# Identity products in TensorE's prologue, and new lists of steps, in a four-batch RWKV decoder layer

## The chip, the cores and the metric

The kernel runs on one core of one Trainium2 chip. The metric is the device time of one execution in microseconds (us). The kernel before was run three times: 599.24, 600.77 and 601.04 us, median 600.77. One further execution was taken by the profiler. It took 598.28 us, and the span from its first to its last instruction is 596.4 us.

## The reference, cut to what matters

For each of 4 batches of 512 tokens with 512 features, three residual blocks follow each other:

```python
x = x + _L0_attn_ref(_layernorm(x), Wk, Wv, Wr, Wo, tm_k, tm_v, tm_r, time_decay, time_first, ln_g, ln_b)
x = x + _L0_xattn_ref(4, 512, 512, w, u, _layernorm(x), ctx_2048)
x = x + _L0_ffn_ref(_layernorm(x), gate_w, up_w, down_w, gate_s, up_s, down_s)
```

The first block mixes each token with the one before it, projects it with Wk, Wv and Wr, runs the stabilised RWKV recurrence over the tokens (`out = (e1*aa + e2*vt) / (e1*bb + e2)` with running maximum), normalises, gates with the sigmoid of r and projects with Wo. The second runs a like recurrence with the normalised x as key and the context as value. The third is a gated feed-forward layer of 1408 inner features.

## The kernel before

Everything is in one launch, in float32. Each engine has a written list of steps for four stages: `*_FIRST` (the prologue: batch 0, and with a `+` behind the name the first half of batch 1), `*_BODY` (a hardware loop of two rounds), `*_NEXT` and `*_LAST`. In a round the feed-forward part of batch b-1, the second half of batch b's attention work and the first half of batch b+1's run interleaved. An engine runs its list strictly in order. It waits for the others only through semaphores, so a step that is not ready holds up all steps behind it on its engine.

The names that the prediction uses, with their lines:

- PE (TensorE): `turn1` to `turn4` and `return2` and `y` are 16 (for `turn4_0`, `turn4_1`: 8) transposes of 128x128 (L625, L675). `k0` to `k3`, `v0`.., `r0`.. are projections of one block of 128 features over 512 tokens (L636), `wo` is the output projection of all four token blocks (L698). `up0` to `up21` (L722) and `down0` to `down21` (L650) are the feed-forward part. `flag` (L706) is one product whose result chooses the form of the main loop.
- DVE (VectorE): `stat1_k` are the statistics of one half of a batch's x (L980), `stat2_k` those of the recurrence's output (L933), `normN` normalises one block of tokens (L946, L988), `mixk`, `mixv`, `mixr` (L963), `front` (L1014 to L1022), `nv`, `den`, `num`, `part`, `fin` are the recurrence (L1035, L1028, L1041, L1046, L954 and L956), the same with an x in front belong to the second block, `x1_t` and `xf_t` are the residual sums (L1067, L1116), `z4` (L1123) makes the low part of the feed-forward input, `prod` (L1128) and `rest` (L973) belong to the feed-forward part.
- ACT (ScalarE): `share_k` copies and scales a turned block (L778, L810), `rw` scales the normalised output for the gate (L853), `tanh`, `silu`, and `weigh0` to `weigh5`, which sum the low halves of the feed-forward weights.
- SP issues all transfers, on one queue. `words0` to `words2` load gate, up and down from their copies in HBM (L529), each after its copy has landed. `xload0+` and `xload1+` load the two halves of batch 1's x into `mixv` (L494), from which `stat1_0+`, `stat1_1+`, `norm0+`, `norm1+` and `turn1+` start the whole first half of batch 1.

The PSUM banks are four, and are used in turn in the order of PE's list: each use waits until the reader of the use four before it is done. The free accumulators are `gu` (two, for `up`) and `dacc` (two, for `down`).

Of the kernel before, what the change touches and what calls it, by code (L numbers as in the profile page):

```python
# [44 lines left out]
def decoder_layer(nc, x, ctx_t, wk_t, wv_t, wr_t, wo_t, vecs_in, gate_t, up_t, down_t, ffn_scales, down_s, out):  # L45
# [22 lines left out]
    PE_FIRST = """
        turn1 k0 k1 v0 v1 k2 k3 v2 v3 r0 r1 r2 r3 turn2 return2 turn1+ k0+ k1+ v0+ wo v1+ turn3 r0+ r1+
        r2+ r3+ y k2+ k3+ v2+ v3+ turn4_0 flag  # L70
# [33 lines left out]
        norm0 rw2 rw3 norm1 share_k0 share_k1 share_k2 share_k3 share_v0 high2 silu6 silu7 share_v1
        share_v2 share_v3 front0 front1 part0 share_r0 share_r1 sq4 share_r2 share_r3 sq5 high3 norm4
        norm5 part1 silu8 silu9 front2 front3 high4 silu10 silu11 silu12 high5 silu13 part2 part3 silu14
        silu15 high6 xfront0 high7 xfront1 silu16 silu17 xpart0 high8 xpart1 xfront2 xfront3 silu18
        silu19 tanh0 tanh1 tanh2 tanh3 xpart2 high9 xpart3 silu20 silu21 high10 sq6 norm6 z4_0_0 z4_0_1
# [3 lines left out]
        sq7 norm7 silu0 silu1 z4_1_0 z4_1_1 silu2 high0 silu3 high1 norm2 norm3 rw0 rw1 rw2 rw3 silu4  # L112
        sq4 silu5 norm4 high2 sq5 silu6 silu7 norm5 xfront0 xfront1 silu8 silu9 xpart0 high3 silu10
        high4 silu11 xpart1 high5 silu12 silu13 xfront2 xfront3 silu14 high6 silu15 high7 silu16 silu17
        silu18 silu19 xpart2 xpart3 high8 silu20 silu21 high9 sq6 high10 norm6 z4_0_0 z4_0_1
# [11 lines left out]
        nv3 part2 den3 num3 part3 fin2 fin3 stat2_0 stat2_1 norm2 norm3 stat1_0+ stat1_1+ norm0+ rw0 rw1
        rw2 norm1+ mixk0+ mixk1+ mixk2+ mixk3+ mixv0+ mixv1+ mixv2+ mixv3+ front0+ rw3 front1+ den0+
        mixr0+ mixr1+ mixr2+ mixr3+ nv0+ num0+ part0+ den1+ x1_0 x1_1 x1_2 x1_3 fin0+ norm4 nv1+ norm5
        num1+ xfront0 part1+ xin0 xden0 fin1+ xnum0 xfront1 xpart0 xin1 xden1 xfin0 xnum1 xfront2 xpart1  # L130
        xden2 xin2 xfin1 xnum2 xfront3 xpart2 xin3 xden3 xnum3 xpart3 xfin2 xfin3 xf_0 xf_1 xf_2 xf_3
# [16 lines left out]
        norm7 prod0 z4_1_0 z4_1_1 prod1 prod2 stat2_0 stat2_1 prod3 rest0 norm2 norm3 rw0 rw1 rw2 rw3
        prod4 x1_0 x1_1 prod5 norm4 x1_2 rest1 rest2 x1_3 norm5 prod6 prod7 xfront0 xfront1 xin0 xden0
        xnum0 xin1 prod8 prod9 xpart0 xden1 xnum1 rest3 xpart1 prod10 prod11 xfin0 rest4 xfront2 rest5  # L150
        xfin1 prod12 prod13 xfront3 out0 out1 xin2 prod14 prod15 xden2 rest6 xnum2 prod16 rest7 prod17
        xpart2 xden3 prod18 xin3 xnum3 prod19 xpart3 xfin2 xfin3 rest8 xf_0 xf_1 rest9 prod20 prod21
# [1040 lines left out]
```

## Time and profile before

| | us |
|---|---|
| median of three runs | 600.77 |
| the profiled execution | 598.28 |
| its span | 596.4 |
| prologue, to the first `up` | 165.3 |
| first and second round of the loop | 136.7 each |
| `*_NEXT`, to the first `up` of `*_LAST` | 87.5 |
| `*_LAST` with the end | 70.2 |

The boundaries of the stages are the starts of `up0` on PE. "Busy" is the time in which an engine works, and the PEclk column of the windows is the granted TensorE clock as a share of 2.4 GHz: 0.50 is 1.2 GHz.

### The profile page before, as it was taken

What the parts mean: (1) busy time and instruction counts of PE and PEld (TensorE: products, weight loads), DVE (VectorE), ACT (ScalarE), POOL (GpSimd) and SP (SyncE); (2) the same over time, 40 slices, a digit from 0 to 9 for tenths busy, and PEclk for the clock granted to TensorE, in tenths of its full rate; (3) what the DMA queues carried; (4) which work ended last, traced back from release to release, by engine and by line L of the source; (5) the groups of instructions that cost most, each with busy time, mean ns of one, the idle gap of its engine ahead of it and who ended that gap; (6) DMA issues with size and microseconds to landing.
All of it is one profiled execution on the core that took longest, in us unless ns stands there. A gap on an engine that the chain in (4) does not pass through costs nothing.

```text
span 596.4 us, 8018 instructions
## 1 busy us (share of the span) xinstructions
PE 536.3 (90%) x2658; PEld 381.6 (64%) x2658; DVE 457.1 (77%) x742; ACT 345.4 (58%) x546; POOL 53.4 (9%) x155
## 2 busy tenths in 40 slices
PE   2998589677799999999889999999969999999995
PEld 2443444323398446885689446786768699989994
DVE  5999778996977489999857589999856499852433
ACT  4737783467868257676557447766644486634221
POOL 2000300101022003000103003000011100000000
PEclk9999699988989999999979999999979999999998
DMA  8999700012100000001060000001040010010001
GB/s 304 414 315 385 291 0 2 18 35 87 48 26 2 1 1 0 1 19 53 1 213 0 0 0 1 0 18 53 0 142 0 1 38 36 0 36 1 2 36 38
DMA packets 14261, 39.02 MB, mean 65 GB/s; under 512 B 1232, under 2 KB 1232, under 8 KB 14032
## 3 DMA queue, kind: packets, MB, share of 16 engines
q1 hardware_dynamic: 14224, 38.57, 18.0%
q8 instruction: 18, 0.29, 0.2%
q14 instruction: 19, 0.16, 0.1%
HBM read 34.37 MB, written 12.85 MB: 79 GB/s over the span
## 4 chain that ended last, share of the span: by engine, by line
issue 38%; PE 34%; DVE 15%; POOL 6%; ACT 5%; DMA 1%; DVEq 0%; POOLq 0%; SPq 0%; ACTq 0%
PE gu L722 13%; PE dacc L650 7%; PE bank L636 6%; PE bank L698 5%; PE bank L625 3%; POOL t_rstd L598 2%; DVE t_slot L954 2%; DVE t_st L1091 1%; ACT L745 1%; DVE t_slot L1099 1%; DVE t_otile L1149 1%; DVE t_slot L1046 1%; POOL t_veps L596 1%; ACT t_z L799 1%; DVE t_xf L1116 1%
## 5 line engine op out<-in xcount | busy, mean ns | idle before, releaser
L722 PE MATMUL gu<-t_z4h,t_gate 128*128 128x256 f32 x352 | 94.1, 299 | 7.9 <-DVE t_z4l L1123 7.5
L722 PE MATMUL gu<-t_z4l,t_gate 128*128 128x256 f32 x352 | 89.3, 286 | 0.0
L722 PE MATMUL gu<-t_z4l,t_up 128*128 128x256 f32 x352 | 89.3, 286 | 0.0
L722 PE MATMUL gu<-t_z4h,t_up 128*128 128x256 f32 x352 | 89.2, 285 | 0.0
L879 ACT ACTIVATE t_h<-gu,t_fsc 128x256 f32<-128x256 f32 x88 | 40.4, 472 | 67.3 <-PE gu L722 65.8
L722 PEld LDWEIGHTS gu<-t_z4h,t_gate 128*128 128x128 f32 x352 | 68.4, 194 | 12.7 <-issue 10.4
L650 PE MATMUL dacc<-t_down,t_hh 128*128 128x512 f32 x176 | 72.5, 412 | 1.8 <-DVE t_hl L973 1.8
L722 PEld LDWEIGHTS gu<-t_z4l,t_gate 128*128 128x128 f32 x352 | 68.3, 194 | 2.4 <-issue 1.7
L650 PE MATMUL dacc<-t_down,t_hl 128*128 128x512 f32 x176 | 69.0, 392 | 0.0
L1128 DVE SCALAR_TENSOR_TENSOR t_h<-gu,t_fsc,t_h 128x256 f32<-128x256 f32 x88 | 40.6, 476 | 36.0 <-ACT t_h L879 35.9
L722 PEld LDWEIGHTS gu<-t_z4h,t_up 128*128 128x128 f32 x352 | 68.1, 193 | 0.0
L722 PEld LDWEIGHTS gu<-t_z4l,t_up 128*128 128x128 f32 x352 | 68.0, 193 | 0.0
L636 PE MATMUL bank<-t_mixk,t_wk 128*128 128x512 f32 x128 | 58.6, 607 | 3.6 <-DVE t_mixk L963 3.3
L745 ACT ACT_TABLE_LOAD x45 | 57.7, 1283 | 1.5 <-PEq L1187 0.7
L636 PE MATMUL bank<-t_mixv,t_wv 128*128 128x512 f32 x128 | 56.7, 592 | 0.0
L698 PE MATMUL bank<-t_wo,t_tanh_r 128*128 128x512 f32 x128 | 55.6, 592 | 0.0
L636 PEld LDWEIGHTS bank<-t_mixk,t_wk 128*128 128x128 f32 x128 | 24.0, 193 | 35.8 <-issue 28.8
L636 PEld LDWEIGHTS bank<-t_mixv,t_wv 128*128 128x128 f32 x128 | 24.3, 190 | 29.0 <-issue 28.7
L698 PEld LDWEIGHTS bank<-t_wo,t_tanh_r 128*128 128x128 f32 x128 | 24.1, 190 | 29.4 <-issue 28.2
L954 DVE TENSOR_TENSOR t_slot<-t_slot 128x1024 f32<-128x1024 f32 x32 | 38.9, 1216 | 2.5 <-ACT t_slot L866 1.4
L650 PEld LDWEIGHTS dacc<-t_down,t_hh 128*128 128x128 f32 x176 | 33.1, 188 | 11.0 <-issue 5.5
L761 ACT ACTIVATE t_hh<-t_h 128x512 fp32r<-128x512 f32 x44 | 27.5, 625 | 20.0 <-PE dacc L650 10.1
(129 smaller groups left out, 930.5 us busy)
## 6 DMA issues: line engine op xcount, KB each, us to landing
t_mixv<-in_x SPq DMA_DIRECT2D x8, 512.0 KB, 6.0
t_xres<-in_x SPq DMA_DIRECT2D x8, 512.0 KB, 5.5
t_ctxt<-in_ctx_t SPq DMA_DIRECT2D x16, 256.0 KB, 2.8
out<-t_otile SPq DMA_DIRECT2D x16, 256.0 KB, 2.2
gate_words<-in_gate_t SPq DMA_DIRECT2D x1, 2816.0 KB, 17.1
up_words<-in_up_t SPq DMA_DIRECT2D x1, 2816.0 KB, 24.3
t_gate<-gate_words SPq DMA_DIRECT2D x1, 2816.0 KB, 15.5
down_words<-in_down_t SPq DMA_DIRECT2D x1, 2816.0 KB, 23.1
```

Of the source, the lines that this page charges most:

```text
L596: pool.tensor_tensor(veps[:, half(k)], var[:, half(k)], small[:, EPSILON, half(k)], ALU.add).then_inc(veps_done, 1)
L598: pool.tensor_tensor(rstd[:, half(k)], veps[:, half(k)], small[:, MINUS_HALF, half(k)], ALU.pow).then_inc(rstd_done, 1)
L625: done = pe.transpose(bank_of(b, s, m)[:, k * P:(k + 1) * P], src[:, k, m * P:(m + 1) * P], ident[:, :])
L636: last = pe.matmul(bank_of(b, s, c)[:, :], w[:, k, c * P:(c + 1) * P], src[:, k, :], start=(k == 0), stop=(k == C - 1))
L650: last = pe.matmul(dacc[j][:, :], as_read(part[:, u % 4, j * P:(j + 1) * P], exact), as_read(down[:, i, :], exact), start=(i == 0 and part ...
L698: done = pe.matmul(bank_of(b, s, m)[:, :], tanh_r[:, k, m * P:(m + 1) * P], wo[:, k, :], start=(k == 0), stop=(k == C - 1))
L722: last = pe.matmul(gu[u % 2][:, side, :], as_read(w[:, k, i * P:(i + 1) * P], exact), as_read(part[:, k, hf * HALF:(hf + 1) * HALF], exact ...
L745: act.preload_act_table_set(name)
L761: act.activation(pair(hh, p), pair(h, p), ACT.Copy).then_inc(hh_done, 1)
L879: act.activation(h[:, u % 4, :], gu[u % 2][:, 0, :], ACT.Silu, scale=fsc[:, 0, u % NI:u % NI + 1]).then_inc(silu_done, 1)
L954: dve.tensor_tensor(slot[:, c % 2, 2:4, :], both, slot[:, c % 2, 0:1, :].to_broadcast([P, 2, T]), ALU.mult).then_inc(square, 1)
L1128: dve.scalar_tensor_tensor(out=h[:, u % 4, :], in0=gu[u % 2][:, 1, :], scalar=fsc[:, 1, u % NI:u % NI + 1], in1=h[:, u % 4, :], op0=ALU.mu ...
```

## The change

PE's prologue list gets 27 steps `warm0` to `warm26`. Each is five products of the identity with itself, 128x128 in float32, into the accumulator `gu[1]`, which nothing reads there; they wait for nothing beside the identity. All lists of PE, ACT and DVE are laid out anew, in all stages; POOL's `*_NEXT` changes by one swap; on SP `words2` now stands ahead of `xload0+` and `xload1+`, and in the loop the loads of x stand first. DVE's `rw` steps get one more wait, for the `tanh` of the same block. No arithmetic that reaches the output is added or removed.

```diff
     PE_FIRST = """
-        turn1 k0 k1 v0 v1 k2 k3 v2 v3 r0 r1 r2 r3 turn2 return2 turn1+ k0+ k1+ v0+ wo v1+ turn3 r0+ r1+
-        r2+ r3+ y k2+ k3+ v2+ v3+ turn4_0 flag
+        warm0 warm1 turn1 warm2 k0 k1 v0 v1 v2 k2 k3 v3 r0 r1 r2 r3 warm3 turn2 warm4 warm5 warm6 warm7
...
     SP_FIRST = """
-        words1 xload0+ xload1+ words2 ctx2 ctx3
+        words1 words2 xload0+ xload1+ ctx2 ctx3
...
     SP_BODY = """
-        ctx0 ctx1 rload0 rload1 xload0 xload1 ctx2 ctx3 out0 out1 out2 out3
+        xload0 xload1 ctx0 ctx1 rload0 rload1 ctx2 ctx3 out0 out1 out2 out3
...
+                elif kind(s) == "warm":
+
+                    for _ in range(5):
+                        pe.matmul(gu[1][:, 0, 0:P], ident[:, :], ident[:, :], start=True, stop=True)
...
                     need(dve, lnt_done, b, c + 1)
+                    need(dve, tanh_done, b, c + 1)
```

SP's queue in the prologue, after the copies of gate and up have been issued. In brackets stand the semaphores that a transfer waits for; before:

```order
L529 DMA t_gate<-gate_words 128x4x1408 [waits gate_raw]
L525 DMA down_words<-in_down_t 64x11264
L529 DMA t_up<-up_words 128x4x1408 [waits up_raw]
L494 DMA t_mixv<-in_x 128x2x512 [waits newv_done] x2
L529 DMA t_down<-down_words 128x11x512 [waits down_raw]
```

and now:

```order
L532 DMA t_gate<-gate_words 128x4x1408 [waits gate_raw]
L528 DMA down_words<-in_down_t 64x11264
L532 DMA t_up<-up_words 128x4x1408 [waits up_raw]
L532 DMA t_down<-down_words 128x11x512 [waits down_raw]
L497 DMA t_mixv<-in_x 128x2x512 [waits newv_done] x2
```

The two halves of batch 1's x now stand behind the load of down, and behind its wait for the copy of down.

PE from `turn2` of batch 0 to the end of the prologue; the products with `t_ident` alone are the new steps, `t_zt` is the recurrence's output, `t_wo`, `t_wk`, `t_wv`, `t_wr` are the weights. Before:

```order
L625 MATMUL bank<-t_ident,t_zt 128x128 x16
L625 MATMUL bank<-t_ident,t_z 128x128 x16
L625 MATMUL bank<-t_ident,t_mixv 128x128 x16
L636 MATMUL bank<-t_mixk,t_wk 128x512 x8
L636 MATMUL bank<-t_mixv,t_wv 128x512 x4
L698 MATMUL bank<-t_wo,t_tanh_r 128x512 x16
L636 MATMUL bank<-t_mixv,t_wv 128x512 x4
L625 MATMUL bank<-t_ident,t_z 128x128 x16
L636 MATMUL bank<-t_xf,t_wr 128x512 x16
L625 MATMUL bank<-t_ident,t_z 128x128 x16
L636 MATMUL bank<-t_mixk,t_wk 128x512 x8
L636 MATMUL bank<-t_mixv,t_wv 128x512 x8
```

and now, from `return2` on:

```order
L628 MATMUL bank<-t_ident,t_z 128x128 x16
L710 MATMUL gu<-t_ident 128x128 x5
L628 MATMUL bank<-t_ident,t_mixv 128x128 x16
L701 MATMUL bank<-t_wo,t_tanh_r 128x512 x16
L639 MATMUL bank<-t_mixk,t_wk 128x512 x8
L639 MATMUL bank<-t_mixv,t_wv 128x512 x8
L710 MATMUL gu<-t_ident 128x128 x15
L628 MATMUL bank<-t_ident,t_z 128x128 x16
L710 MATMUL gu<-t_ident 128x128 x35
L639 MATMUL bank<-t_xf,t_wr 128x512 x16
L639 MATMUL bank<-t_mixk,t_wk 128x512 x8
L639 MATMUL bank<-t_mixv,t_wv 128x512 x8
```

`wo` moved ahead of `k0+`, and `k2+` to `v3+` moved ahead of `y`, which (with 16 transposes of `t_z`) now follows them, then 25 identity products, `flag`, `turn4_0` and the last 10.

DVE at the second half of `stat2` of batch 0 (`t_stats<-bank`), with batch 1's x in `t_mixv`. Before:

```order
L933 BN_STATS t_stats<-bank 128x6 x2
L938 MEMSET t_scrap 128x1
L940 BN_AGGR t_mv<-t_stats 128x2 x2
L946 TENSOR_SCALAR t_z<-bank,t_rstd,t_nmr 128x512 x2
L980 BN_STATS t_stats<-t_mixv 128x6 x2
```

and now:

```order
L940 BN_STATS t_stats<-bank 128x6 x2
L945 MEMSET t_scrap 128x1
L947 BN_AGGR t_mv<-t_stats 128x2 x2
L987 BN_STATS t_stats<-t_mixv 128x6 x2
L989 MEMSET t_scrap 128x1
L991 BN_AGGR t_mv<-t_stats 128x2 x2
L953 TENSOR_SCALAR t_z<-bank,t_rstd,t_nmr 128x512 x2
```

The statistics of batch 1's first half (`stat1_0+`) now stand ahead of `norm2` and `norm3` of batch 0.

## Rows read from the trace of the kernel before

**Rows 1.** Windows: the stages; busy us (instructions) of each engine, clock, DMA share, GB/s

```profile
60.00:79.00 19.00, 11.00 (x45) 8.89 (x46) 12.03 (x30) 13.15 (x17) 4.92 (x16) 0.64 0.59 221
79.00:107.30 28.30, 28.30 (x66) 12.06 (x67) 24.40 (x38) 18.47 (x33) 2.70 (x7) 1.00 0.00 1
107.30:165.10 57.80, 39.49 (x106) 17.84 (x104) 51.62 (x70) 37.98 (x51) 2.86 (x10) 0.89 0.16 54
165.30:302.00 136.70, 130.68 (x664) 94.22 (x664) 115.81 (x185) 86.70 (x137) 15.08 (x36) 0.97 0.04 13
302.00:438.70 136.70, 130.75 (x665) 94.31 (x665) 112.44 (x181) 83.70 (x135) 14.57 (x36) 0.97 0.09 31
438.70:526.20 87.50, 86.80 (x552) 74.11 (x553) 61.20 (x106) 51.84 (x85) 8.26 (x26) 0.98 0.09 31
```

**Rows 2.** DMA issues: size, median us from issue to landing

```profile
t_up<-up_words SPq DMA_DIRECT2D x1, 2816.0 KB, 22.9
t_down<-down_words SPq DMA_DIRECT2D x1, 2816.0 KB, 17.2
```

**Rows 3.** Timeline of SP's queue: start us, duration of the issue

```profile
38.79 0.38 SPq L529 DMA_DIRECT2D t_up<-up_words  x1
51.86 0.89 SPq L494 DMA_DIRECT2D t_mixv<-in_x  x2
54.53 0.37 SPq L529 DMA_DIRECT2D t_down<-down_words  x1
```

**Rows 4.** The tile `mixv`, 45 to 80 us: landing of batch 1's two halves

```profile
DMA to landing us min/median/max: 11.2/11.7/12.1
```

**Rows 5.** Timeline of DVE around `norm3` and `stat1_0+`, and one scan

```profile
67.11 0.81 DVE L946 TENSOR_SCALAR t_z<-bank,t_rstd,t_nmr 128x512 f32<-128x512 f32 x1 [0.66 <-POOL t_nmr L601]
67.83 1.27 DVE L980 BATCH_NORM_STATS2 t_stats<-t_mixv 128x6 f32<-128x512 f32 x2
69.31 1.25 DVE L980 BATCH_NORM_STATS2 t_stats<-t_mixv 128x6 f32<-128x512 f32 x2
98.61 1.23 DVE L1028 TENSOR_TENSOR_SCAN t_st<-t_fade,t_slot 128x512 f32<-128x512 f32 x1
```

**Rows 6.** Timeline of PE: `return2`, `wo`, `v1+`, `r1+`

```profile
67.97 3.25 PE L625 MATMUL bank<-t_ident,t_z 128*128 128x128 f32 x14 [0.96 <-DVE t_z L946]
89.94 13.90 PE L698 MATMUL bank<-t_wo,t_tanh_r 128*128 128x512 f32 x32
103.67 3.60 PE L636 MATMUL bank<-t_mixv,t_wv 128*128 128x512 f32 x8
117.82 5.40 PE L636 MATMUL bank<-t_xf,t_wr 128*128 128x512 f32 x8 [2.86 <-DVE t_slot L1073]
```

**Rows 7.** Timeline of ACT: `rw0` to `rw3` of batch 0, `share_k0+`

```profile
71.64 2.77 ACT L853 ACTIVATE t_z<-bank,t_half_b,t_half_g 128x512 f32<-128x512 f32 x4
76.89 0.69 ACT L778 ACTIVATE t_mixk<-bank,t_vecs 128x512 f32<-128x512 f32 x1 [1.78 <-PE bank L625]
```

**Rows 8.** Waits of DVE, 107.3 to 165.1 us: us in total, times, longest

```profile
DVE t_slot L1014 <- PE bank L636: 2.9, 1, 2.9
DVE t_slot L954 <- ACT t_slot L866: 1.4, 1, 1.4
```

**Rows 9.** Page, groups: the first part of a `fin`

```profile
L954 DVE TENSOR_TENSOR t_slot<-t_slot 128x1024 f32<-128x1024 f32 x32 | 38.9, 1216 | 2.5 <-ACT t_slot L866 1.4
```

**Rows 10.** Timeline of DVE at the end of the prologue: the flag, `norm7`

```profile
163.77 0.14 DVE L1142 TENSOR_SCALAR t_general<-gu 1x1 int32<-1x1 f32 x1
170.02 0.55 DVE L946 TENSOR_SCALAR t_z<-t_xf,t_rstd,t_nmr 128x512 f32<-128x512 f32 x1 [1.20 <-POOL t_nmr L601]
```

**Rows 11.** Windows: the first 3.9 us of the first round

```profile
165.30:169.20 3.90, 3.89 (x18) 3.90 (x19) 3.45 (x4) 3.87 (x6) 0.94 (x2) 0.50 0.02 6
```

**Rows 12.** Timeline of PE: transposes of `y` in the first round; `up0` of the loop

```profile
289.37 1.47 PE L625 MATMUL bank<-t_ident,t_z 128*128 128x128 f32 x12
165.31 0.55 PE L722 MATMUL gu<-t_z4h,t_gate 128*128 128x256 f32 x1 [2.43 <-DVE t_z4l L1123]
```

More of the change, by code:

```diff
@@ L68, in decoder_layer @@
     PE_FIRST = """
-        turn1 k0 k1 v0 v1 k2 k3 v2 v3 r0 r1 r2 r3 turn2 return2 turn1+ k0+ k1+ v0+ wo v1+ turn3 r0+ r1+
-        r2+ r3+ y k2+ k3+ v2+ v3+ turn4_0 flag
+        warm0 warm1 turn1 warm2 k0 k1 v0 v1 v2 k2 k3 v3 r0 r1 r2 r3 warm3 turn2 warm4 warm5 warm6 warm7
+        warm8 return2 warm9 turn1+ wo k0+ k1+ v0+ v1+ warm10 warm11 warm12 turn3 warm13 warm14 warm15
+        warm16 warm17 warm18 warm19 r0+ r1+ r2+ r3+ k2+ k3+ v2+ v3+ y warm20 warm21 warm22 warm23 warm24
+        flag turn4_0 warm25 warm26
         """.split()
     PE_BODY = """
-        up0 up1 turn4_1 up2 turn2 up3 up4 up5 return2 down0 up6 down1 turn1 up7 wo k0 k1 v0 k2 k3 down2
-        v1 down3 down4 up8 up9 down5 v2 v3 up10 up11 down6 down7 up12 up13 down8 down9 down10 turn3 up14
-        up15 down11 r0 up16 up17 up18 down12 down13 r1 up19 r2 r3 down14 down15 up20 down16 up21 down17
+        up0 up1 turn4_1 up2 turn2 up3 up4 down0 return2 up5 down1 down2 turn1 up6 up7 k0 k1 v0 v1 k2 k3
+        down3 wo v2 v3 up8 r0 r1 r2 down4 turn3 down5 up9 up10 up11 down6 down7 up12 up13 r3 down8 down9
+        down10 up14 up15 up16 down11 down12 down13 up17 up18 up19 up20 down14 down15 down16 up21 down17
         y down18 down19 down20 down21 turn4_0
@@ L104, in decoder_layer @@
[L104 to L108, printed above, removed]
+        sq7 silu0 norm7 silu1 z4_1_0 z4_1_1 silu2 silu3 high0 norm2 norm3 silu4 high1 rw0 rw1 rw2 rw3
@@ L109, in decoder_layer @@
         """.split()
     ACT_NEXT = """
[L112 to L115, printed above, removed]
+        sq7 norm7 silu0 silu1 z4_1_0 z4_1_1 high0 silu2 silu3 high1 norm2 norm3 silu4 silu5 rw0 rw1 rw2
@@ L127, in decoder_layer @@
[L127 to L131, printed above, removed]
@@ L132, in decoder_layer @@
-        front2+ norm6 front3+ den2+ nv2+ num2+ part2+ nv3+ den3+ num3+ weigh part3+ flag z4_0_0 z4_0_1
-        fin2+ fin3+
+        stat1_0 stat1_1 norm0 norm1 mixk0 mixk1 mixk2 mixk3 mixv0 mixv1 mixv2 mixv3 front0 front1 nv0
+        den0 num0 nv1 part0 mixr0 den1 fin0 num1 front2 mixr1 part1 nv2 mixr2 mixr3 fin1 front3 den2
+        num2 nv3 part2 den3 num3 part3 fin2 fin3 stat2_0 stat2_1 stat1_0+ norm2 norm3 stat1_1+ norm0+
+        norm1+ rw0 rw1 rw2 rw3 mixk0+ mixk1+ mixk2+ mixk3+ mixv0+ x1_0 x1_1 mixv1+ mixv2+ mixv3+ mixr0+
@@ L134, in decoder_layer @@
+        mixr1+ mixr2+ mixr3+ x1_2 x1_3 norm4 front0+ norm5 front1+ den0+ nv0+ num0+ part0+ nv1+ den1+
+        num1+ part1+ fin0+ xfront0 fin1+ xin0 xfront1 xden0 xnum0 xin1 xpart0 xden1 xnum1 xpart1 xfin0
+        xfront2 xfin1 xin2 xfront3 xden2 xnum2 xpart2 xin3 weigh xden3 xnum3 xpart3 xfin2 xfin3 front2+
+        front3+ den2+ nv2+ nv3+ num2+ xf_0 xf_1 part2+ xf_2 den3+ num3+ norm6 xf_3 part3+ flag z4_0_0
+        z4_0_1 fin2+ fin3+
         """.split()
     DVE_BODY = """
-        norm7 prod0 z4_1_0 z4_1_1 prod1 prod2 rest0 stat2_0 stat2_1 prod3 norm2 norm3 stat1_0 prod4
@@ L143, in decoder_layer @@
-        xfront2 xfin1 xfront3 rest7 rest8 xin2 xden2 xnum2 prod18 xpart2 xin3 xden3 xnum3 prod19 xpart3
-        rest9 xfin2 xfin3 prod20 prod21 xf_0 xf_1 rest10 out2 norm6 xf_2 out3 z4_0_0 xf_3 z4_0_1
+        norm7 prod0 prod1 z4_1_0 z4_1_1 prod2 stat2_0 stat2_1 prod3 rest0 norm2 norm3 stat1_0 stat1_1
+        rest1 norm0 norm1 prod4 prod5 mixk0 mixk1 mixk2 mixk3 rw0 mixv0 mixv1 rw1 front0 mixv2 mixv3
+        front1 den0 nv0 num0 part0 rw2 rw3 den1 nv1 num1 part1 mixr0 mixr1 fin0 front2 fin1 front3 x1_0
@@ L145, in decoder_layer @@
         """.split()
     DVE_NEXT = """
[L148 to L152, printed above, removed]
+        norm7 prod0 z4_1_0 z4_1_1 prod1 prod2 stat2_0 stat2_1 prod3 rest0 norm2 norm3 rest1 rw0 rw1 rw2
```

68 lines of the change are left out of this document (39 added, 29 removed).

## The prediction

> **What bounds the kernel now.** I read the windows by stage first [rows 1]. In the two rounds of the loop PE is busy for 130.7 of 136.7 us, in the next stage for 86.8 of 87.5 us: there PE is the bound, and a new order can only win back 6.0 us a round. The prologue is another matter. From 79.0 to 107.3 us PE never rests, from 107.3 to 165.1 us DVE is busy for 51.6 of 57.8 us and PE for 39.5, and from 60 to 79 us no engine is above 13.2 of 19 us, with the clock at 0.64: a chain that goes back and forth between DVE, POOL, ACT and PE. Its waits name what the change aims at: after 107.3 us DVE waits 2.9 us once for a projection (L1014 [rows 8]), since `y` stands ahead of `k2+`, and 1.4 us for ACT.
>
> **What the clock costs now.** PE's 14 transposes of `return2` take 3.25 us, 0.23 each [rows 6]; 12 in the loop take 1.47 us, 0.12 each [rows 12]. The first window of the loop is at 0.50, 1.2 GHz, after 2.4 us of rest [rows 11, 12]. At full clock it would save half of 3.9 us, 1.9 us. After a rest of 2.86 us, 8 passes of `r1+` take 5.40 us, against 3.60 [rows 6].
>
> **The price of the 27 groups.** No row shows an identity product. A float32 product goes through PE in two passes (the 16 products of `wo` are 32 rows); 8 passes of 512 columns start within 103.67 - 89.94 = 13.73 us / 32 each, 0.43 us, so 128 columns cost 0.107 us, and a transpose of that width 0.12. A group of ten passes is 1.1 us at full and 2.2 us at half clock: I take 1.1. All 27 are 30 us of PE, hidden where PE waits anyway; each is followed below.
>
> **The sum, step by step.** Times are of the profiled execution (598.28 us, span 596.4), which is 2.5 us under the median of the runs.
>
> 1. *Batch 1's x comes later.* Before, up landed at 38.79 + 22.9 = 61.7 us, the halves of x at 51.86 + 11.2 = 63.1 and about 52.3 + 12.1 = 64.4, down at 54.53 + 17.2 = 71.7 us [rows 2 to 4]. So the one queue delivers in the order of issue, and down took 7.3 us of it. `words2` can't be issued before 54.53, as it waits for its copy. With x behind it, down lands at 61.7 + 7.3 = 69.0 and x at 70.4 and 71.7 us.
>
> 2. *DVE waits there, with batch 0 behind it.* `turn2` ends near 61 to 63 us, and two `stat2` steps of 1.5 us are done by 66 even at half clock, so all that the new order and `warm3` gain before it is lost in this wait. `stat1_0+` starts at 70.4, takes 69.31 - 67.83 = 1.5 us, then `norm2` and `norm3` follow: 71.9 and 72.6, done at 73.4 us. Before, `norm3` was done at 67.9 [rows 5]. That is 5.5 us late. `warm4` to `warm8` (5.5 us) lie in the hole and cost nothing; after them PE rests for some 6 us, so `return2` is at half clock again.
>
> 3. *To `share_k0+`.* `return2` 3.3 us, four `rw` on ACT 2.7 us [rows 6, 7]: 79.5 us; `warm9` lies beside the `rw` steps. Then come the last nine or ten transposes of `turn1+`: 1.1 us at full clock, 2.3 at half. 80.6 to 81.8; in the middle 81.2, against 76.89 before [rows 7]: 4.3 us late, so 1.2 have come back.
>
> 4. *`wo` first.* `wo` needs the turned blocks 0 and 1, 2.3 us on, then 15 products of 0.86 us, then four projections of 3.43 us: `v1+` ends 28.9 us after `share_k0+`, at 110.1 us; before, at 103.67 + 3.43 = 107.1. DVE stands idle for the `wo` result and for `k0+` meanwhile, which before it did not need to.
>
> 5. *From `nv1+` to the feed-forward input.* Before, this part had 51.6 us of DVE work in 57.8 [rows 1]. Now `den1+` (1.2) and `fin0+` (1.2 + 0.7) are still to come [rows 5, 9] and `norm5` (0.5) is done: 54.2 us. The waits of 2.9 and 1.4 us go, since `k2+` to `v3+` now come ahead of `y`. PE has room: `turn3` ends near 115, `warm13` to `warm19` (7.7 us) near 122.5, and the last `r+` waits for DVE near 134 in any case; four projections behind it end near 152, when DVE needs `v3+` near 153. With 0.5 us of small gaps the low part is ready at 110.1 + 54.2 + 0.5 = 164.8 us; before 165.1. The 5.5 us of loss and the reordering's gain cancel.
>
> 6. *Into the loop.* `turn4_0` is followed by `warm25` and `warm26`, 2.2 us, which end with the low part. But the read of the flag's result stands behind them in PE's queue, and from that result (163.77 + 0.14 [rows 10]) to `up0` (165.31 [rows 12]) took 1.4 us. So `up0` starts near 166.1, 0.8 us late, at full clock. It then saves 1.9 us, of which most is lost again at `turn4_1`, behind `up1`: it needs `norm7`, done at 170.6 us [rows 10], whose own chain from `xf_3` is about as late as before. Net -0.2 us (-1 to +1).
>
> 7. *Loop, next, last.* The work is the same, PE's rest is 6.0 us a round, nearly all at the end of it, in the chain from `y` over `xf_1` and `norm6` to `up0`; that chain keeps its steps. Walking the new lists, `down0` and `return2` come close behind their inputs (I count 1 us of new waits a round) and the 0.7 us around `y` and the last `down` steps go. I take +0.2 a round (-1.5 to +1.5), -0.1 for the rest. The wait added to `rw` is always met: ACT did `tanh` long before.
>
> Sum: -0.2 + 0.4 - 0.1 = +0.1 us: 598.4 us for a profiled execution, 600.9 as a median. This kernel's runs differ by 0.3%, 1.8 us, so that is the bound of "same". The likeliest case's own range is 599.0 to 602.6.
>
> **Rivals.**
>
> *A. x is not held up* (0.10). If the two transfers share the engines in another manner, or down is copied earlier, the 5.5 us of step 2 go, and with them the half clock of `return2` (14 x 0.11 = 1.6 us) and the wait of up to 1.2 us in step 3: about 8.3 us faster, 592.5. For it speaks only that nothing else in the new order is placed as if x were late; against it all four landings [rows 2 to 4]. The Trainium skill ("DMA: Bandwidth & Descriptors", Queues, rings and completion order) says that transfers of one issuing engine need not complete in the order of issue. No landing of this trace shows that.
>
> *B. The new order gains in the loop* (0.23). The 6.0 us of rest a round shrink by 1.5, the clock in step 6 gives its whole 1.9: -3.0 - 1.7 = -4.7, 596.0; half of that is enough for "faster". For it: DVE is at 115.8 and 112.4 of 136.7 us, so its order has room [rows 1].
>
> *C. Groups at half clock in the way* (0.25, the other side). Ahead of `y` PE waits for `nv2+` and `nv3+` with no group to bridge it, about 2.5 us, as long as the rest that brought 1.2 GHz before `r1+` [rows 6]. Then `y` takes 1.5 us more, and `warm20` to `warm24`, begun late and up to 2.2 us each until the clock is back, end 2 us after `norm6` is ready; `turn4_0` stands behind them. With step 3 at its upper end (+0.6) and 1 us of small waits: +3.6, 604.5. It decides from +1.8 us, when the groups end 1.2 us too late.
> The Trainium skill ("TensorE: Matmul & The Clock Gate", Part 4, PE-mode transpose) says that transposes do not count as busy for the clock. The trace leans to it: clock 0.64 over 60 to 79 us with PE busy 11.0 of 19 us, mostly on transposes [rows 1]. Here that rule would put step 3 at 81.8 and the total at 601.5.
>
> *D. As summed* (0.42).
>
> **Chances.** Faster by over 0.3%: A, B and little else, 0.33. Same 0.42. Slower: C, 0.25. The range of 8 in 10 leaves out A's end and C's upper tail: 595.0 to 604.5.
>
> **What the changed profile would show.** SP's queue: x issued near 55, landing near 70 and 72. DVE: `stat1_0+` waits some 6 us for the transfer of x, `norm3` near 72.6; if it starts near 64, step 1 is wrong and A holds. ACT: `share_k0+` near 81. PE: `v1+` ends near 110, no wait of DVE for `k2+`, groups of 1.1 us, `up0` near 166 with PEclk 1.00 in the first 4 us. The rounds: 136 to 138 us. If `turn4_0` starts right behind the last group of `warm24`, more than 1 us after `norm6`, C holds.

## The result, and the profile after

| | before | after |
|---|---|---|
| median of 20 runs each, us | 599.83 | 602.11 |
| lowest to highest | 597.96 to 601.82 | 600.55 to 606.52 |
| ratio, 95% interval | | 1.0047 [1.0032, 1.0062] |
| the profiled execution, its span | 598.28, 596.4 | 602.58, 600.7 |

The kernel after is slower by half a per cent, 2.8 us by the ratio (the two medians lie 2.3 us apart). The time lies inside the range, but on the side of rival C, beyond what counts as "same". Laid over each other at the starts of `turn4_1` and `turn4_0`, the two profiles split the 4.3 us by which they differ (more than the runs as a whole do, as the profiled execution of before was 1.5 us under its median):

| stretch | before | after | difference |
|---|---|---|---|
| start to `turn4_1` of round 1 | 170.94 | 173.30 | +2.4 |
| to `turn4_1` of round 2 | 136.64 | 136.91 | +0.3 |
| to `turn4_1` of `*_NEXT` | 136.58 | 136.51 | -0.1 |
| to its `turn4_0` | 79.07 | 80.25 | +1.2 |
| to the end | 73.2 | 73.7 | +0.5 |

The timeline of SP's queue, after, against [rows 3] (start, duration of the issue):

```profile
39.06 0.38 SPq L532 DMA_DIRECT2D t_up<-up_words  x1
54.87 0.37 SPq L532 DMA_DIRECT2D t_down<-down_words  x1
55.28 5.49 SPq L497 DMA_DIRECT2D t_mixv<-in_x  x2
```

The timeline of DVE, after, where batch 0's recurrence output is normalised, against [rows 5]:

```profile
63.39 0.15 DVE L947 BATCH_NORM_AGGREGATE t_mv<-t_stats 128x2 f32<-128x6 f32 x1
70.79 1.29 DVE L987 BATCH_NORM_STATS2 t_stats<-t_mixv 128x6 f32<-128x512 f32 x2 [7.25 <-DMA t_mixv<-in_x]
72.28 1.50 DVE L953 TENSOR_SCALAR t_z<-bank,t_rstd,t_nmr 128x512 f32<-128x512 f32 x2
```

DVE stands still for 7.25 us until the transfer of x, and `norm2` and `norm3` (L953), whose statistics were done at 63.5 us, stand behind it in the list.

The timeline of PE, after, in the prologue, against [rows 6]. `gu<-t_ident` are the new groups (10 rows are one group), L628 the transposes, L701 `wo`, L729 `up0`:

```profile
59.14 1.64 PE L628 MATMUL bank<-t_ident,t_zt 128*128 128x128 f32 x13 [1.74 <-ACT t_tanh_r L835]
60.62 5.75 PE L710 MATMUL gu<-t_ident 128*128 128x128 f32 x50
73.20 3.88 PE L628 MATMUL bank<-t_ident,t_z 128*128 128x128 f32 x16 [6.83 <-DVE t_z L953]
76.87 1.58 PE L710 MATMUL gu<-t_ident 128*128 128x128 f32 x10
82.62 1.67 PE L701 MATMUL bank<-t_wo,t_tanh_r 128*128 128x512 f32 x3 [1.03 <-ACT t_zt L817]
...
103.44 7.03 PE L639 MATMUL bank<-t_mixv,t_wv 128*128 128x512 f32 x16
110.30 3.51 PE L710 MATMUL gu<-t_ident 128*128 128x128 f32 x30
...
156.27 1.64 PE L628 MATMUL bank<-t_ident,t_z 128*128 128x128 f32 x13 [0.80 <-DVE t_slot L1042]
157.75 5.75 PE L710 MATMUL gu<-t_ident 128*128 128x128 f32 x50
163.42 0.19 PE L713 MATMUL gu<-t_ones,t_inexact 128*1 128x1 f32 x2
164.76 1.09 PE L678 MATMUL bank<-t_ident,t_z 128*128 128x128 f32 x8 [1.15 <-DVE t_z L953]
165.69 2.40 PE L710 MATMUL gu<-t_ident 128*128 128x128 f32 x20
167.88 0.35 PE L729 MATMUL gu<-t_z4h,t_gate 128*128 128x256 f32 x1
```

Where PE kept going, transposes take 0.12 us (13 in 1.64); behind the rest of 6.83 us, 16 take 3.88. The windows of after, against [rows 1] and [rows 11] (columns as there):

```profile
82.60:110.30 27.70, 27.68 (x64) 12.17 (x65) 21.26 (x36) 23.33 (x36) 4.75 (x10) 1.00 0.00 1
110.30:167.80 57.50, 52.01 (x276) 35.29 (x275) 55.14 (x73) 36.26 (x51) 4.13 (x7) 1.00 0.16 51
167.80:171.80 4.00, 4.00 (x35) 3.90 (x33) 3.55 (x4) 3.95 (x7) 0.78 (x2) 1.00 0.16 57
167.90:303.30 135.40, 128.90 (x666) 92.60 (x664) 117.52 (x185) 89.33 (x140) 12.95 (x36) 1.00 0.05 14
303.30:440.20 136.90, 130.13 (x664) 93.89 (x665) 113.96 (x181) 86.75 (x139) 12.60 (x36) 0.99 0.09 31
440.20:529.90 89.70, 88.37 (x553) 75.24 (x553) 61.01 (x106) 48.40 (x81) 8.17 (x26) 0.97 0.09 30
```

One thing in the loop has no counterpart before. The timelines of DVE and PE, after, at the start of round 2 (`norm7`, `turn4_1`):

```profile
309.53 0.55 DVE L953 TENSOR_SCALAR t_z<-t_xf,t_rstd,t_nmr 128x512 f32<-128x512 f32 x1 [6.32 <-issue]
310.21 1.09 PE L678 MATMUL bank<-t_ident,t_z 128*128 128x128 f32 x8 [1.56 <-DVE t_z L953]
```

POOL's last input for `norm7` (`t_nmr`, L604) was written from 305.53 us for 0.20, so DVE began some 4 us after it could have. "issue" is time for which the profile shows no wait. Before, DVE stood idle for 2.65 us ahead of the same step, until POOL.

### The profile page after: what moved, and what is told of

Its sections match the earlier page's. It is cut to its first block, busy times and chain, and to the rows that moved or that the text cites. A ratio compares the mean times of both kernels' runs of the same rounds, so it can differ in the third digit from the quotient of the medians.

```text
span 600.7 us, 8573 instructions
## 1 busy us (share of the span) xinstructions
PE 558.3 (93%) x2928; PEld 409.7 (68%) x2928; DVE 460.3 (77%) x742; ACT 347.5 (58%) x548; POOL 52.4 (9%) x155
## 4 chain that ended last, share of the span: by engine, by line
PE 43%; issue 22%; DVE 16%; DMA 9%; ACT 3%; POOL 3%; SPq 2%; DVEq 0%; POOLq 0%; ACTq 0%
PE gu L729 16%; PE dacc L653 9%; PE bank L639 8%; PE bank L701 7%; DMA down_words<-in_down_t 4%; PE bank L628 4%; DMA gate_words<-in_gate_t 3%; DMA t_mixv<-in_x 3%; DVE t_slot L961 2%; POOL t_rstd L601 1%; DVE t_slot L1021 1%; DVE t_st L1099 1%; DVE t_otile L1157 1%; DVE t_slot L1042 1%; DVE t_st L1035 1%
## 5 line engine op out<-in xcount | busy, mean ns | idle before, releaser
L729 PE MATMUL gu<-t_z4h,t_gate 128*128 128x256 f32 x352 | 92.0, 294 | 6.3 <-DVE t_z4l L1131 5.5
L729 PE MATMUL gu<-t_z4l,t_gate 128*128 128x256 f32 x352 | 89.2, 286 | 0.0
L729 PE MATMUL gu<-t_z4h,t_up 128*128 128x256 f32 x352 | 88.5, 284 | 0.0
L729 PE MATMUL gu<-t_z4l,t_up 128*128 128x256 f32 x352 | 88.5, 284 | 0.0
L729 PEld LDWEIGHTS gu<-t_z4h,t_gate 128*128 128x128 f32 x352 | 67.9, 193 | 9.3 <-issue 7.1
L729 PEld LDWEIGHTS gu<-t_z4l,t_gate 128*128 128x128 f32 x352 | 68.0, 193 | 1.5 <-issue 0.7
L729 PEld LDWEIGHTS gu<-t_z4h,t_up 128*128 128x128 f32 x352 | 67.6, 192 | 0.0
L729 PEld LDWEIGHTS gu<-t_z4l,t_up 128*128 128x128 f32 x352 | 67.5, 192 | 0.0
L701 PE MATMUL bank<-t_wo,t_tanh_r 128*128 128x512 f32 x128 | 56.2, 596 | 1.0 <-ACT t_zt L817 1.0
L639 PE MATMUL bank<-t_mixk,t_wk 128*128 128x512 f32 x128 | 56.9, 595 | 0.2 <-DVE t_mixk L970 0.2
L701 PEld LDWEIGHTS bank<-t_wo,t_tanh_r 128*128 128x128 f32 x128 | 23.9, 190 | 31.1 <-issue 28.3
L980 DVE TENSOR_TENSOR t_hl<-t_h,t_hh 128x512 fp32r<-128x512 f32 x44 | 30.1, 685 | 13.8 <-ACT t_hh L768 13.4
```

What stands on the lines that cost most here:

```text
L639: last = pe.matmul(bank_of(b, s, c)[:, :], w[:, k, c * P:(c + 1) * P], src[:, k, :], start=(k == 0), stop=(k == C - 1))
L701: done = pe.matmul(bank_of(b, s, m)[:, :], tanh_r[:, k, m * P:(m + 1) * P], wo[:, k, :], start=(k == 0), stop=(k == C - 1))
L729: last = pe.matmul(gu[u % 2][:, side, :], as_read(w[:, k, i * P:(i + 1) * P], exact), as_read(part[:, k, hf * HALF:(hf + 1) * HALF], exact ...
L980: dve.tensor_tensor(pair(hl, p), pair(h, p), pair(hh, p).bitcast(F32), ALU.subtract).then_inc(hl_done, 1)
```

## The experiments

The kernels ran in three sets of four, each beside the kernel before on the same chip (medians of before 599.91, 599.63 and 600.73 us); after itself had run apart from them, beside a before of 599.83 us. Kernels of different sets are compared by their ratios to before. A ratio is uncertain by 0.15 to 0.35%, so a difference of two ratios by 0.3 to 0.5%, 2 to 3 us. The first set took the change apart.

**e1_x_first: only SP's prologue list as before.**

```diff
-        words1 words2 xload0+ xload1+ ctx2 ctx3
+        words1 xload0+ xload1+ words2 ctx2 ctx3
```

> The changed kernel with the old order of SP's prologue alone: x of batch 1 ahead of the load of down. Theory (the queue): the wait of 7.25 us of VectorE for x goes, stat1_0+ starts near 64, and the start of the first up falls from 167.9 to about 160; in all 7 to 8.5 us faster than the changed kernel, 1.1 to 1.4% less of the time before, so near 594 and about 0.9% below the kernel before. Rival (the wait moves): wo ahead of k0+ and the steps behind it leave VectorE waiting anyway, and less than 3 us come back, so the kernel is still no faster than before.

594.84 us, ratio 0.9927 [0.9893, 0.9961]. Against after that is 1.20%, 7.2 us. The timelines of DVE and PE, same places:

```profile
64.08 1.29 DVE L987 BATCH_NORM_STATS2 t_stats<-t_mixv 128x6 f32<-128x512 f32 x2 [0.30 <-DMA t_mixv<-in_x]
66.50 0.41 PE L628 MATMUL bank<-t_ident,t_z 128*128 128x128 f32 x2
159.71 0.36 PE L729 MATMUL gu<-t_z4h,t_gate 128*128 128x256 f32 x1
```

The wait for x is 0.30 us in place of 7.25, and `up0` starts 8.2 us earlier. One swap in a queue of transfers turned a slower kernel into a faster one.

**e2_no_warm: after without the 27 groups.**

```diff
-        warm0 warm1 turn1 warm2 k0 k1 v0 v1 v2 k2 k3 v3 r0 r1 r2 r3 warm3 turn2 warm4 warm5 warm6 warm7
+        turn1 k0 k1 v0 v1 v2 k2 k3 v3 r0 r1 r2 r3 turn2
...
```

> The changed kernel without the 27 groups of identity products; all else as changed. Theory (the groups are hidden, and what the clock gives back before the loop is lost in waits for VectorE): within 1 us of the changed kernel, ratio to before 1.003 to 1.007; the first up0 and up1 run at 1.2 GHz again (5.5 us instead of 3.8) and turn4_1 waits less. Rival one (the clock pays): 2 us or more slower than the changed kernel, ratio 1.008 or more. Rival two (groups stand in the way, warm20 to warm26 above all): 2 us or more faster, ratio 1.001 or less.

606.38 us, ratio 1.0106 [1.0074, 1.0138]: the groups save 0.59%, 3.5 us (4.3 between the medians). `wo` starts at 84.25 us (after: 82.62), `up0` at 170.74 (167.88), and the passes of `up` run at 1.2 GHz until 176.4. My theory, that the groups are within 1 us of nothing, fell.

**e3_old_loop: after's prologue, and the lists of the loop, next and last stage of before** (all `*_BODY`, `*_NEXT`, `*_LAST`).

```diff
     PE_BODY = """
-        up0 up1 turn4_1 up2 turn2 up3 up4 down0 return2 up5 down1 down2 turn1 up6 up7 k0 k1 v0 v1 k2 k3
+        up0 up1 turn4_1 up2 turn2 up3 up4 up5 return2 down0 up6 down1 turn1 up7 wo k0 k1 v0 k2 k3 down2
...
```

> The changed kernel's prologue, with the lists of the loop, of the next and of the last stage as before. Theory (the new order costs behind the loop): the profile showed rounds 1.0 us shorter and 0.2 longer, the next stage 2.1 and the last 0.6 us longer, so about 2 us faster than the changed kernel, ratio 1.001 to 1.002. Rival (those differences are the clock's and one late fetch of instructions, which come with any list): within 0.7 us of the changed kernel, ratio 1.004 to 1.006.

604.12 us, ratio 1.0069 [1.0042, 1.0095]. That is above the theory's range and, by less than the interval, above the rival's. The new lists don't cost; by the ratios they gain 1.3 us, by overlapping intervals perhaps nothing.

**e4_before_x_last: the kernel before with after's order of SP.**

```diff
-        words1 xload0+ xload1+ words2 ctx2 ctx3
+        words1 words2 xload0+ xload1+ ctx2 ctx3
```

> The kernel before, with the new order of SP's prologue alone: down's load ahead of batch 1's x. Theory (the queue): x lands near 70.4 and 71.7 instead of 63.1 and 64.4; VectorE reaches stat1_0+ at 67.8, so that it waits 2.6 to 3 us, and that chain is the one that ends last there: 2 to 3 us slower than before, ratio 1.0035 to 1.005. Rival (slack behind it): the wait of 3 us is taken up by later rests of VectorE, and the ratio is 1.000 to 1.002.

604.76 us, ratio 1.0067 [1.0041, 1.0093], +4.0 us, more than I expected. The timelines of DVE and PE:

```profile
72.09 1.29 DVE L980 BATCH_NORM_STATS2 t_stats<-t_mixv 128x6 f32<-128x512 f32 x2 [4.47 <-DMA t_mixv<-in_x]
76.81 1.05 PE L625 MATMUL bank<-t_ident,t_mixv 128*128 128x128 f32 x2 [5.89 <-ACT t_z L853]
83.27 1.19 PE L636 MATMUL bank<-t_mixk,t_wk 128*128 128x512 f32 x1 [1.50 <-DVE t_mixk L963]
```

Even where `norm2` and `norm3` stand ahead of `stat1_0+`, `k0+` begins 4.3 us late (83.27; before 79.00, the bound of two windows in [rows 1]), since `norm1+` and all of `turn1+` come after x. In after the same swap cost 7.2 us; the new order of DVE, with `norm2` and `norm3` behind the wait, is the likely rest of it. That is argued from the two timelines: no run has after with the old order of these steps alone.

The second set asked on what the groups and the lists rest.

**e5_x_first_no_warm: e1 without the 27 groups** (the diffs of e1 and e2 together).

> Kernel after with x of batch 1 loaded ahead of down, and without the 27 groups. Theory (the groups pay through the clock, wherever the holes are): without them the kernel with x first loses what the kernel after lost, 606.4 - 602.1 = 4.3 us: 594.8 + 4.3 = 599.1 (597.8 to 600.5), return2 and the first ups of the loop at 0.22 and 0.21 us a pass. Rival (the groups pay only because the late x makes a hole of 7 us): the loss is at most 2 us, 596.8, and the first pass of the loop runs at full clock without them.

600.13 us, ratio 1.0008 [0.9986, 1.0031]. Against e1 the groups are worth 0.81%, 4.9 us: more than in after, so they don't live on the hole that the late x makes. The windows of e5 where PE had only transposes to do (`return2`, `turn1+`), and of the start of `wo`:

```profile
67.00:77.40 10.40, 8.23 (x32) 6.22 (x32) 5.69 (x13) 5.59 (x9) 1.75 (x6) 0.50 0.37 137
77.40:84.00 6.60, 6.57 (x10) 2.91 (x11) 3.68 (x5) 6.57 (x10) 0.00 (x0) 0.64 0.00 0
```

Its timeline of PE, `return2` and the start of `wo`:

```profile
66.92 3.88 PE L627 MATMUL bank<-t_ident,t_z 128*128 128x128 f32 x16 [4.93 <-DVE t_z L952]
77.43 2.90 PE L700 MATMUL bank<-t_wo,t_tanh_r 128*128 128x512 f32 x3 [0.72 <-ACT t_zt L816]
```

PE is busy for 8.23 of 10.4 us with transposes, and the clock stays at 0.50 throughout and into `wo`. `v1+` ends at 107.3 us; in e1 at 102.1. (By the Trainium skill, "TensorE: Matmul & The Clock Gate", Part 4, a transpose does not count as busy for the clock in the same way as other products; this window agrees.)

**e6_x_first_old_loop: e1 with the loop, next and last lists of before** (the diffs of e1 and e3 together).

> Kernel after with x first, its prologue and groups, but all lists of the loop, the next and the last stage as before. Theory (the new lists of the loop are worth 1 to 2 us, as the comparison in the kernel after said weakly): 594.8 + 1.3 = 596.1 (595.3 to 597.3). Rival (they are worth nothing, and the difference there was chance): 594.8 (594.0 to 595.3). If they cost, as the stage NEXT suggests (89.7 against 87.5 us): 593.

594.57 us, ratio 0.9912 [0.9878, 0.9947]. The lists are worth nothing that this can tell (e1: 0.9927).

**e7_before_new_loop: the kernel before with the new loop, next and last lists, and the added wait.**

```diff
+                    need(dve, tanh_done, b, c + 1)
...
-        up0 up1 turn4_1 up2 turn2 up3 up4 up5 return2 down0 up6 down1 turn1 up7 wo k0 k1 v0 k2 k3 down2
+        up0 up1 turn4_1 up2 turn2 up3 up4 down0 return2 up5 down1 down2 turn1 up6 up7 k0 k1 v0 v1 k2 k3
...
```

> Kernel before, whole prologue as it was, with the new lists of the loop, the next and the last stage. Theory (worth 1 to 2 us): 598.6 (597.8 to 599.3), with NEXT at 89.7 us again if its loss lies in the list. Rival (nothing): 599.9. If the loss of NEXT (first ups at 1.2 GHz for 6.3 us in place of 3.6) is chance of the moment at which the clock comes back, NEXT is 87.5 to 88.5 here.

601.12 us, ratio 1.0018 [0.9998, 1.0038]: no gain. The added wait is in this kernel too, so what the lists gain and what the wait costs cannot be told apart in its time. The stretch from `turn4_1` to `turn4_0` of the next stage is 80.27 us again, as in after, e1 and e5 (80.25 to 80.30); with the old list it is 79.04 to 79.07 (before, e3, e6): the new `*_NEXT` list costs 1.2 us. From `turn4_1` of the first round to the next `up0` the new list of the loop takes 130.03 to 130.07 us (e7, after, e1), the old one 131.09 to 131.41 (before, e6, e3): it gains 1.0 to 1.4 us a round. What is left of a round, from `up0` to `turn4_1`, takes 5.5 us before and 6.5 to 6.9 us in after. It hangs on the clock and, in round 2 of after and e7, on the wait for `norm7`. Here I found what I had not looked for. The window of the first 6.3 us of the next stage, before:

```profile
438.66:445.00 6.34, 6.34 (x41) 6.34 (x41) 1.03 (x2) 2.84 (x7) 1.08 (x3) 0.71 0.69 242
```

and after:

```profile
440.21:446.50 6.29, 6.29 (x31) 6.29 (x32) 1.03 (x2) 1.77 (x4) 1.08 (x3) 0.53 0.66 240
```

Same instructions, same rest of 2.5 and 2.7 us ahead of them, but the clock comes back 3.7 us after `up0` in one and 5.9 us after it in the other, which costs 1.1 us. The moment at which it fell differs likewise: in before it had been at 1.2 GHz since 3.1 us ahead of `up0`, in after only since 0.9 us ahead of it.

**e8_before_warm: the kernel before with 16 groups in its own rests, and the added wait.**

```diff
-        turn1 k0 k1 v0 v1 k2 k3 v2 v3 r0 r1 r2 r3 turn2 return2 turn1+ k0+ k1+ v0+ wo v1+ turn3 r0+ r1+
-        r2+ r3+ y k2+ k3+ v2+ v3+ turn4_0 flag
+        warm0 warm1 turn1 warm2 k0 k1 v0 v1 k2 k3 v2 v3 r0 r1 r2 r3
+        warm3 turn2 warm4 warm5 return2 warm6 turn1+ k0+ k1+ v0+ wo v1+ turn3 r0+ warm7 warm8 r1+
+        warm9 r2+ warm10 warm11 r3+ y k2+ k3+ v2+ v3+ turn4_0 warm12 warm13 flag warm14 warm15
...
+                    need(dve, tanh_done, b, c + 1)
```

> Kernel before with nothing changed but 16 groups put into its PE list at its own rests (three around turn1, one ahead of turn2, two ahead of return2, one behind it, two ahead of r1+, one ahead of r2+, two ahead of r3+, two ahead of flag and two behind it). Theory (the clock alone pays): return2 saves 1.6 us, the tenths of turn1+ and r1+, r3+ that ran at half clock about 1, the first ups of the loop 1.9: 599.9 - 3.5 = 596.4 (595.4 to 597.6). Rival (DVE is the bound of the prologue, so that only the first ups count): 598.0 (597.3 to 599).

598.17 us, ratio 0.9972 [0.9946, 0.9999]: the rival's number. But the profile shows nearly the theory's gain, lost again later: `turn4_1` of round 1 starts at 167.82 us, 3.1 earlier than before, and the next two rounds take 138.2 each in place of 136.6. Step by step round 1 is that of before within 0.1 us up to `up0`, and then:

```profile
305.23 0.55 DVE L952 TENSOR_SCALAR t_z<-t_xf,t_rstd,t_nmr 128x512 f32<-128x512 f32 x1 [6.40 <-issue]
306.00 1.09 PE L677 MATMUL bank<-t_ident,t_z 128*128 128x128 f32 x8 [0.90 <-DVE t_z L952]
```

(timelines of DVE and PE). The late start of `norm7` is there again, in a kernel whose lists of DVE are those of before. It is in all nine kernels with the added wait (after, e1 to e3, e5 to e9; 5.6 to 7.1 us of "issue"), and not in before and e4 (2.65 and 2.64 us, until POOL). The third set tried that.

**e10_before_warm_no_wait: e8 without the added wait.**

```diff
                     need(dve, lnt_done, b, c + 1)
-                    need(dve, tanh_done, b, c + 1)
```

> Kernel before with the 16 groups in its PE list, as in the last call, but without the added wait of DVE's rw steps for tanh, so that DVE's program is word for word that of before. In all runs with that wait DVE's first step of the second round (norm7) began 5.6 to 7.1 us after the step ahead of it, though its input was there; without it, in the kernel before, after 2.7. Theory (the wait lengthens DVE's loop and its jump back costs more): idle time 2.7 us again, no wait of turn4_1 in round 2, 598.2 - 0.9 = 597.3 (596.3 to 598.0). Rival (it comes of the groups or of the moment of the jump): 598.2, idle time over 5.5 us.

595.52 us, ratio 0.9922 [0.9899, 0.9946], against e8's 0.9972: 0.50%, 3.0 us (2.7 between the medians), and faster than the whole range of the theory. So 16 groups in the old order, without the wait, are worth 0.78%, 4.7 us, under before. The timeline of DVE:

```profile
301.17 0.55 DVE L952 TENSOR_SCALAR t_z<-t_xf,t_rstd,t_nmr 128x512 f32<-128x512 f32 x1 [2.64 <-POOL t_nmr L603]
```

The step starts when POOL is done, and PE no longer waits for it. The page counts 8337 instructions, with the wait 8353: 16 more, one for each `rw` step of the four batches. The wait never waited, but it is an instruction of its own.

The traces show more of what stands ahead of `norm7`. In e8, the branch at the end of DVE's loop, its first instruction behind the jump (both of L454), and the DMA queues from 303.4 to 305.2 us:

```profile
L454 DVEq COMPARE_BRANCH  x1: 73/73/73, 297.3 to 297.3; - x1
L454 DVEq FUSED_REGOPS  x1: 74/74/74, 300.9 to 300.9; - x1
q14 instruction: 1, 0.01, 1.5%
```

The last line is one packet of 8 KB of instructions. Such packets stand in the same places in all 14 kernels. The first starts 1.0 to 1.7 us after DVE's branch, and DVE's next instruction comes 2.9 to 3.7 us after the branch, where the other engines take 0.2 to 0.3 us. A second starts some 2 to 3.5 us later. In the nine kernels with the added wait `norm7` begins 1.8 to 1.9 us after the start of this second packet (e8: 303.5 and 305.23 us); in the five without it begins 1.7 to 2.6 us ahead of it (e10: 301.17 and 303.7 us). So in the nine `norm7` seems to wait until the next piece of DVE's program has come. That is read from these places in time: the profile does not name the packet as what `norm7` waited for.

**e12_x_first_no_wait: e1 without the added wait** (the same line).

> Kernel after with x first, all groups and all new lists, only without the added wait of DVE's rw steps for tanh. Theory (the wait lengthens DVE's jump back, but turn4_1 did not wait for it here, as the clock was low until then): idle time ahead of norm7 in round 2 falls from 5.9 to about 2.3 us, time 594.7 (594.0 to 595.4). Rival (the wait is free in every respect): idle time stays at 5.9. Second rival (the jump costs time on the path): 593.7.

592.89 us, ratio 0.9881 [0.9857, 0.9905], against e1's 0.9927: 0.46%, 2.8 us (2.0 between the medians). The timeline of DVE:

```profile
298.08 0.55 DVE L953 TENSOR_SCALAR t_z<-t_xf,t_rstd,t_nmr 128x512 f32<-128x512 f32 x1 [2.55 <-POOL t_nmr L604]
```

The idle time fell as expected, 5.86 to 2.55 us. The time fell by more than I expected and by more than the profiled spans show (592.2 to 591.0). In e1 `turn4_1` had not waited for `norm7` at all.

**e11_best: e12 with the next and last lists of before.**

```diff
     PE_NEXT = """
-        up0 up1 turn4_1 up2 turn2 up3 up4 up5 return2 down0 down1 wo up6 up7 up8 turn3 up9 up10 down2
+        up0 up1 turn4_1 up2 turn2 up3 up4 up5 return2 down0 down1 wo up6 up7 turn3 up8 down2 up9 down3
...
```

> Kernel after with x first, without the added wait, and with the lists of the next and the last stage as before; the new list of the loop stays. Theory (from turn4_1 to turn4_0 the new list of the next stage took 80.25 us in four kernels, the old 79.05): 594.8 - 1.2 = 593.6 (592.8 to 594.5). Rival (the loop with the old and the new lists measured the same, so single stages say nothing): 594.7 (594.3 to 595.5).

592.15 us, ratio 0.9863 [0.9840, 0.9887], the fastest of all: 1.37% under before and 1.84%, 11 us, under after. The stretch to `turn4_0` of the next stage is 79.05 us, 1.2 less than in e12; in the time the step is 0.18%, below what the intervals tell apart. The median is below the theory's range, which had been counted from e1 and had put the wait at about nothing.

**e9_x_first_six_groups: e1 with `warm4` to `warm9` alone.**

```diff
-        warm0 warm1 turn1 warm2 k0 k1 v0 v1 v2 k2 k3 v3 r0 r1 r2 r3 warm3 turn2 warm4 warm5 warm6 warm7
+        turn1 k0 k1 v0 v1 v2 k2 k3 v3 r0 r1 r2 r3 turn2 warm4 warm5 warm6 warm7
...
```

> Kernel after with x first, and of the 27 groups only six: warm4 to warm8 ahead of return2, and warm9 behind it. Without any group v1+ ended at 107.3 us and turn4_1 of the first round began at 171.7, with all of them at 102.1 and 165.1: 5.2 of the 6.6 us were lost between return2 and the first products of wo. Theory (these six carry nearly all): 594.8 + 1.3 = 596.1 (595.3 to 597.2), v1+ ends near 102. Rival (the clock is a matter of the whole stretch, and the groups at the loop's start count as much): 598.3 (597.3 to 599.5).

597.92 us, ratio 0.9947 [0.9928, 0.9965]. The median alone is nearer to the rival. By the ratio, as the other comparisons of different sets are made, it is 596.7 us beside e1's before, which is inside the theory's range: six groups bring 0.61% of the 0.81% that all 27 bring (e5 to e1), and what they lack, 0.20%, is within the intervals. In the profiled spans (e5 598.9, e9 596.6, e1 592.2 us) they bring only a third. How much of the gain the six carry stays open. The timeline of PE:

```profile
60.52 3.04 PE L627 MATMUL bank<-t_ident,t_zt 128*128 128x128 f32 x13 [2.81 <-ACT t_tanh_r L834]
63.34 7.28 PE L709 MATMUL gu<-t_ident 128*128 128x128 f32 x50
70.47 1.91 PE L627 MATMUL bank<-t_ident,t_z 128*128 128x128 f32 x16
```

Its windows of the same stretch:

```profile
60.50:63.30 2.80, 2.79 (x13) 2.79 (x14) 1.04 (x2) 2.49 (x2) 0.00 (x0) 0.50 1.02 405
63.30:70.40 7.10, 7.10 (x52) 7.10 (x51) 6.93 (x23) 2.37 (x3) 3.56 (x12) 0.77 1.05 388
70.40:78.00 7.60, 5.61 (x46) 4.82 (x44) 3.82 (x7) 4.89 (x8) 1.31 (x4) 1.00 0.14 51
```

Without `warm3` ahead of it `turn2` meets 1.2 GHz, the five groups begin late and at half clock, take 7.1 us in place of 5.6, and hold `return2` up until 70.47 us (e1: 66.50). From there on the clock is 1.00, and `v1+` ends at 105.6 us. So in this profile the groups hang together as a chain: the early ones keep the later ones short. I had treated them as independent. What the chain is worth in time, these runs do not tell.

## Why the prediction was right or wrong, by its steps

**Steps 1 to 4 came out nearly to the tenth.** x was there by 70.8 us (70.4), `norm2` started at 72.28, `return2` ran at half clock, and two later values were:

```profile
81.30 0.69 ACT L785 ACTIVATE t_mixk<-bank,t_vecs 128x512 f32<-128x512 f32 x1 [0.70 <-PE bank L628]
```

(timeline of ACT, after: `share_k0+`, forecast 81.2) and `v1+`, which ended at 110.3 (110.1). The mechanism, x held up by the queue, is shown by e1: its price is 7.2 us. Rival A had priced the same mechanism from the other side, at 8.3. A group costs 1.12 us (three between 110.30 and 113.65), as priced.

**Step 5 is where the profiled execution lost its 2.4 us.** It set 54.2 us of DVE work and 0.5 of gaps behind `v1+`'s end; the window shows 55.14 busy and 2.36 idle, of which 1.1 is a wait of `norm6` for POOL. "The 5.5 us of loss and the reordering's gain cancel" was false by 2.9 us: the low part was ready at 167.7, not at 164.8.

**Step 6.** `up0` started right behind the last group (167.88 us; forecast 166.1), so the read of the flag does not stand in its way, against what I had said; it is the late low part of step 5 that makes it late. Full clock came as forecast (1.00 in [rows 11]'s place), and most of it was lost at `turn4_1`, which waits 1.40 us for `norm7`, as said.

**Step 7.** The sum of the two rounds was right (+0.2 in all, forecast +0.4), by errors that cancel: the new list gains 1.0 to 1.4 us a round, where I had counted a small loss, and `up0` to `turn4_1` takes 1.3 and 1.0 us longer than before, by the late `norm7` and, in the next stage, the clock's later return. The last two stages cost 1.7 us (forecast -0.1): 1.2 of it is the new `*_NEXT` list.

**The term put at nothing.** The end of step 7 says: "The wait added to `rw` is always met: ACT did `tanh` long before." It is always met, and it costs 2.8 us in e12 and 3.0 us in e10, each uncertain by 2 to 2.5 us. Taken off by these numbers, after would stand near +0.0 us, the forecast of case D; that is an estimate, since after without the wait was not run.

**How much of it was luck.** It was not this one term that was wrong. By the profiles the sum missed by +2.6 us up to `turn4_1` of round 1 (step 5's "cancel"), by -0.2 in the rounds, where the unforeseen gain of the list met the cost that showed there, and by +1.8 behind them. The range held because it is 9.5 us wide and because, in the rounds, a gain and a cost that I had not foreseen cancel. And 602.11 us lies even in the likeliest case's own range of 599.0 to 602.6 only because the forecast started from a median of 600.77 for before, 0.9 us above that of the twenty runs; the ratio of 1.0047 is outside what case D said.

**Rivals.** C's mechanism did not occur in after: its groups ahead of `turn4_0` ran at full clock and ended 1.15 us before it. It is real, though, and e9 shows it elsewhere, where the groups before it are missing. The time came out on C's side for other reasons. B's gain in the loop, 1.5 us a round, was put about right for the list itself (1.0 to 1.4, e7's stretches), and did not reach the end.

**In the ratios:** x behind down +1.20% (e1), the wait +0.46% (e12), the groups -0.59% (e2), and the sum is +0.47%; so -0.6%, 3.6 us, is left for the new order, with -0.22% or +0.15% of it from the lists behind the prologue (e3, e6). The rest, which no run has by itself, would be the new prologue order. This adds up terms that were measured in different kernels, and it is not firm: e5, which has the new order everywhere, the wait, x first and no groups, stands at 1.0008, which less the wait's 0.46% gives the new order only -0.38%.

**What stays open** is how the wait's 2 to 3 us come about. Shown: 16 more instructions; the late start of `norm7` after the jump back, gone in the three kernels from which the wait was taken (e10, e11, e12), and the packet of instructions ahead of it. In the profiles this accounts for 0.9 us of e8's 3.1 (the wait of `turn4_1`) and for none of e1's 1.2. The other part lies in when the clock comes back behind the rests ahead of `up0`: over rounds 2 and the next stage 3.5 to 4.1 us after `up0` in before, e4 and e10, 3.8 to 5.4 in e11 and e12, and 2.8 to 6.0, on average 5.2, in the nine kernels with the wait. Over all runs the mean granted clock is the same with and without the wait (e8 0.975 and e10 0.976, e1 and e12 0.980), so the wait does not noticeably lengthen the time at 1.2 GHz; it could still shift it from rests into work. Whether it does, or it was chance in the profiled executions, I cannot say. Nor did I try the line at another place, or padding of the same length.
The Trainium skill ("Runtime: NRT & Kernel Launch", Instruction fetch mechanics) says that a taken branch whose target is out of the fetched window stalls until it has been fetched. The traces agree: DVE's next instruction comes 2.9 to 3.7 us behind its branch, with a packet of instructions in that time.
